# Attention heads on one core: V sums in two banks, later row maxima, a 128-row bias, and turned batch loops

## The chip, the cores and the metric

One core of a Trainium2 chip runs the whole program. The metric is the device time of one execution in microseconds, as the median over the runs that are shown. A shorter time is better. The core has five engines that run their own instruction streams and meet only at semaphores: TensorE (PE in the profile), VectorE (DVE), ScalarE (ACT), GpSimd (POOL) and SyncE (SP), which here only issues transfers.

## The reference, cut to what matters

The input is 8 sequences of 1024 rows of 256 numbers. A first layer (a selective scan, with its layer norm) is not touched by the change. The second layer is:

```
qkv = x @ W_qkv + b_qkv            # 16 heads of 16 columns
p = softmax(q @ k.T / sqrt(16))    # per head, 1024 x 1024
attn_out = p @ v
gate = softmax(x @ W_gate + b_gate); keep the two largest of 8
moe_out = sum_e gate_e * (x @ W_experts[e] + b_experts[e])
x = layernorm(x + attn_out + moe_out)
```

## The kernel before, in words

The kernel has two phases. The scan takes the first half of the time. The attention phase then goes through 8 batches (one sequence each), and each batch has an experts stage and a heads stage. Each engine has a Python-unrolled body for these stages inside a hardware loop over batches: `experts(0)` stands ahead of the loop, the loop body is `heads(b)` and then `experts(b + 1)`, and the last `heads` stands behind it. On VectorE the loop over heads 1 to 13 is a hardware loop as well.

**A step** is one head. It has eight rounds, `kt` 0 to 7. In a round TensorE makes the two halves of the transposed scores of key tile `kt` (`scores_t`, L1043) into two PSUM banks by turns, and ScalarE turns each half into probabilities (`exp_unit`, L1247). Beside them TensorE makes the untransposed scores of the head two steps ahead (`scores`, L1026), of which VectorE takes the row maxima (`take_max`, L1372). The sums of probabilities times V (`weigh_v`, L1056) accumulate over the eight key tiles in PSUM bank 6. Tiles 0 to 4 are summed in rounds 3 to 7 of the head's own step. Tiles 5 to 7 are late: tile 5 is summed in round 0 of the next step, tiles 6 and 7 both in round 1.

**The sums on their way out.** ScalarE copies the finished sums of the head before out of PSUM (`take_o`, L1254) after the first exponential of round 2. TensorE turns them in round 6 (`turn_o`, L1068) into bank 7, and VectorE divides by the row sums (`normalise`, L1379 and L1381). Since bank 6 is the only one for sums, `weigh_v` of tile 0 waits until `take_o` is done.

**The maxima on their way in.** The row maxima of the next head must be subtracted inside the score matmul, as two more rows of `q_st`. TensorE turns them (`turn_max`, L1035) at the end of round 3 into bank 7. ScalarE copies them (`take_max`, L1260) after the first exponential of round 4. SyncE then issues four small transfers of `m_rows` into `q_st` (L948). The first `scores_t` of the next step waits for all four (semaphore `s_md`, L1041).

**The experts stage.** TensorE makes 32 units of six 512-column matmuls each (L1163). ScalarE scales the odd units (L1305) and GpSimd adds them (L1006), VectorE adds the even ones (L1494 to L1504). Behind sixteen of the units 13 to 31 (the tuple `EARLY`) TensorE also makes one tile of scores of heads 0 and 1 (L1026), and VectorE takes its maxima. At the end ScalarE waits for the last GpSimd sum before its first exponential, since both use the same memory.

**The projections** of the next batch (`qk_proj`, L1088) run inside steps 14 and 15. Each half ends with a matmul of two rows (L1090) that adds the bias.

Of the kernel before, what the change touches and what calls it, by code (L numbers as in the profile page):

```python
# [24 lines left out]
P = 128  # L25
NB = 8
# [719 lines left out]
def attention_phase(nc, d):  # L746
    with ExitStack() as ctx:
# [50 lines left out]
        b_one = sb("b_one", [2, HALF], F16)  # L798
# [15 lines left out]
        r_sum = sb("r_sum", [P, 2, QUARTERS, 1])  # L814
# [79 lines left out]
        EARLY = tuple(u for u in range(13, EU) if u % 2 or u in (16, 20, 22, 24, 26, 28))  # L894
# [5 lines left out]
        block = ctx.enter_context(nc.Block())  # L900

# [76 lines left out]
        def _(pool):  # L978
# [4 lines left out]
            pool.memset(b_one[:, :], Q_UP)  # L983
            pool.memset(eps_col[:, :], EPS).then_inc(s_const, 1)
            pool.wait_ge(s_const, 1)
            pool.memset(k_st[QR - HD:RG, :, :], Q_UP).then_inc(s_const, 1)
# [28 lines left out]
        def _(pe):  # L1015
# [15 lines left out]
            def turn_max(b, h, normalised):  # L1031

                pe.wait_ge(s_nm, normalised + 1)
                pe.wait_ge(s_mp, b * HEADS + h + 1)
                pe.transpose(ps[0:2 * TT, 7, 0:P], m_parts[:, :, :].rearrange("p c t -> p (c t)"), ident[:, :]).then_inc(s_mt, 1)  # L1035
# [10 lines left out]
            def weigh_v(b, h, kt):  # L1046

                g = b * HEADS + h
                pe.wait_ge(s_p, g * (2 * TT) + (2 * kt + 4))
                if kt in (0, 5):  # L1050
                    pe.wait_ge(s_vh, g * 2 + (1 + kt // 5))
                if kt == 0:
                    pe.wait_ge(s_o, g + 1)
                n = T // QUARTERS
                for j in range(QUARTERS):
                    mm = pe.matmul(ps[VC * j:VC * (j + 1), 6, 0:n], v_h[:, kt, :], probs[:, kt, j * n:(j + 1) * n],  # L1056
                                   start=(kt == 0), stop=(kt == TT - 1), skip_group_check=True)
                mm.then_inc(s_pv, 1)

            def turn_o(b, h, turned=False):  # L1060

                g = b * HEADS + h
                if turned:
                    pe.wait_ge(s_mr, g + 4)
                pe.wait_ge(s_o, g + 2)
                pe.wait_ge(s_nm, g + 1)
                for i in range(2):
                    mm = pe.transpose(ps[:, 7, i * P:(i + 1) * P], o_sb[:, i * P:(i + 1) * P], ident[:, :])  # L1068
                mm.then_inc(s_ot, 1)
# [10 lines left out]
            def qk_proj(b, n, half):  # L1080

                mt = SEQ[n]
                if n == 0:
                    pe.wait_ge(s_xte, (b + 1) * KH)
                if n >= 2:
                    pe.wait_ge(s_parts, b * (2 * KH) + (n - 1))
                for i, (k, w, x) in enumerate(TERMS):
                    pe.matmul(ps[:, 2 * (n % 2) + half, :], w_qk[:, w, k, mt * P:(mt + 1) * P],  # L1088
                              x1T[:, x, k, half * HALF:(half + 1) * HALF], start=(i == 0), stop=False)
                mm = pe.matmul(ps[:, 2 * (n % 2) + half, :], b_st[0:2, mt * P:(mt + 1) * P], b_one[:, :], start=False, stop=True)  # L1090
                if half == 1:
                    mm.then_inc(s_qk, 1)
# [12 lines left out]
            def step(b, h, before, ahead, front):  # L1105
# [3 lines left out]
                for kt in range(TT):  # L1109
# [40 lines left out]
            def experts(b):  # L1150
                for t in range(4, TT):
                    v_proj(b, t)
                for t in range(TT):
                    for e2 in range(E // 2):
# [3 lines left out]
                        if u == 3:  # L1158
# [7 lines left out]
                        if u in EARLY:  # L1166
                            unit = EARLY.index(u)
# [3 lines left out]
                            for half in range(2):  # L1171
                                scores(b, unit // TT, unit % TT, 1 - half)
                            if unit == TT + 4:
                                turn_max(b, 0, b * HEADS)
# [44 lines left out]
        def _(act):  # L1219
# [30 lines left out]
            def take_o(b, h):  # L1250
# [3 lines left out]
                act.activation(o_sb[:, :], ps[:, 6, 0:T // QUARTERS], ACT.Copy).then_inc(s_o, 1)  # L1254

            def take_max(b, h):
# [3 lines left out]
                act.activation(m_rows[:, :], ps[0:2 * TT, 7, 0:P], ACT.Copy).then_inc(s_mr, 1)  # L1260
# [67 lines left out]
        def _(dve):  # L1328
# [45 lines left out]
            def normalise(b, h):  # L1374
                g = b * HEADS + h
                o = ps[:, 7, 0:2 * P].rearrange("p (i j c) -> p i j c", i=2, c=VC)
                to = att[:, :, ds(h * HD, HD)].rearrange("p (j i) c -> p i j c", i=2)
                dve.wait_ge(s_ot, g + 2)
                dve.reciprocal(r_sum[:, :, :, :], o[:, :, :, HD:HD + 1]).then_inc(s_rc, 1)  # L1379
                dve.wait_ge(s_rc, g + 1)  # L1380
                dve.tensor_tensor(to, o[:, :, :, 0:HD], r_sum[:, :, :, :].broadcast_to([P, 2, QUARTERS, HD]),  # L1381
# [53 lines left out]
            def experts(b, late):  # L1435
# [45 lines left out]
                for t in range(TT):  # L1481
                    if late is not None and t < 4:
                        add_experts(late, 2 * t, 2 * t + 2)
                    for e2 in range(E // 2):
# [14 lines left out]
                        if u in EARLY:  # L1499
                            unit = EARLY.index(u)  # L1500
                            take_max(b, unit // TT, unit % TT, unit >= TT)
# [92 lines left out]
            with dve.Fori(0, NB - 1) as b:  # L1594
                heads(b, True)
                experts(b + 1, b)
# [59 lines left out]
```

## Time and profile before

| | us |
|---|---|
| median of 3 runs | 4483.18 |
| lowest and highest | 4480.59, 4494.94 |
| the profiled execution | 4478.55 |
| its span | 4476.8 |
| PE, DVE, ACT busy | 3758.6, 3393.0, 2626.5 |
| chain of waits: PE | 33% |

The profile is of one execution. Busy times are unions over an engine's instructions. An engine's share of the whole span mixes the scan with the attention phase, so the rows below are of single stretches of the attention phase.

### The profile page before, as it was taken

What the parts mean: (1) busy time and instruction counts of PE and PEld (TensorE: products, weight loads), DVE (VectorE), ACT (ScalarE), POOL (GpSimd) and SP (SyncE); (2) the same over time, 40 slices, a digit from 0 to 9 for tenths busy, and PEclk for the clock granted to TensorE, in tenths of its full rate; (3) what the DMA queues carried; (4) which work ended last, traced back from release to release, by engine and by line L of the source; (5) the groups of instructions that cost most, each with busy time, mean ns of one, the idle gap of its engine ahead of it and who ended that gap; (6) DMA issues with size and microseconds to landing.
All of it is one profiled execution on the core that took longest, in us unless ns stands there. A gap on an engine that the chain in (4) does not pass through costs nothing.

```text
span 4476.8 us, 134619 instructions
## 1 busy us (share of the span) xinstructions
PE 3758.6 (84%) x52938; PEld 1752.8 (39%) x52938; DVE 3393.0 (76%) x3617; ACT 2626.5 (59%) x3840; POOL 1618.4 (36%) x1102
## 2 busy tenths in 40 slices
PE   6888878788877888888578988989889898898987
PEld 4445444454544445444332332323223232232322
DVE  6777767777677777777688788787887878788785
ACT  4545446454554545545228668485785857758587
POOL 4656746567465665756620020201102011020100
PEclk8899989999898998999889999999999999999998
DMA  3333334242342423434250230603205050050500
GB/s 104 106 88 97 101 82 115 78 115 73 97 115 73 115 74 99 121 77 108 79 76 11 44 53 2 95 2 59 39 3 94 2 73 25 18 79 2 83 5 11
DMA packets 143258, 301.00 MB, mean 67 GB/s; under 512 B 24344, under 2 KB 63904, under 8 KB 142432
## 3 DMA queue, kind: packets, MB, share of 16 engines
q1 hardware_dynamic: 142688, 292.60, 29.3%
q8 instruction: 455, 7.45, 0.7%
q14 instruction: 115, 0.94, 0.1%
HBM read 223.32 MB, written 35.13 MB: 58 GB/s over the span
## 4 chain that ended last, share of the span: by engine, by line
PE 33%; ACT 7%; issue 6%; DVE 3%; ACTq 1%; DMA 0%; SPq 0%; POOL 0%; DVEq 0%; POOLq 0%
PE ps L1056 10%; PE ps L1043 10%; PE ps L1163 6%; ACT probs L1247 6%; PE ps L1088 2%; PE ps L1026 1%; PE ps L1068 1%; PE ps L1101 1%; ACT o_sb L1254 1%; PE ps L1189 1%; PE ps L1035 1%; ACT m_rows L1260 1%; PE ps L1090 0%; DVE diag_b L1529 0%; ACTq L1246 0%
## 5 line engine op out<-in xcount | busy, mean ns | idle before, releaser
L335 POOL TENSOR_TENSOR z<-z,c_rep 128x1024 f32<-128x1024 f32 x512 | 1210.2, 2377 | 830.3 <-DVE z L720 829.8
L1247 ACT ACTIVATE probs<-ps,e_scale 128x512 f32<-128x512 f32 x2048 | 1295.5, 683 | 350.7 <-PE ps L1043 320.6
L720 DVE TENSOR_TENSOR_SCAN z<-dA,ps 128x1024 f32<-128x1024 f32 x512 | 1155.1, 2279 | 353.6 <-PE ps L386 333.2
L1372 DVE TENSOR_REDUCE neg_max<-ps 128x1 f32<-128x1024 f32 x1024 | 1236.8, 1222 | 173.5 <-PE ps L1026 145.7
L1043 PE MATMUL ps<-q_st,k_st 50*128 50x512 f16 x2048 | 717.5, 398 | 217.0 <-ACT probs L1247 182.2
L602 ACT ACTIVATE dA<-rep,a_rep 128x1024 f32<-128x1024 f32 x512 | 578.6, 1145 | 526.8 <-DVE z L720 519.4
L386 PE MATMUL ps<-diag,u_t 64*64 64x64 f32 x32768 | 635.5, 231 | 272.4 <-DVE z L720 197.6
L386 PEld LDWEIGHTS ps<-diag,u_t 64*64 64x64 f32 x32768 | 572.3, 144 | 516.0 <-issue 515.0
L1026 PE MATMUL ps<-k_st,q_st 48*128 48x512 f16 x2048 | 689.1, 395 | 0.1
L1056 PE MATMUL ps<-probs,v_h 128*32 128x256 f32 x8192 | 641.7, 399 | 0.0
L1012 POOL COPY v_h<-v_all 128x80 f32 (+1 forms) x256 | 62.2, 245 | 1502.5 <-PE ps L1056 1502.5
L405 PE MATMUL ps<-z,eye 128*64 128x512 f32 x2048 | 518.7, 629 | 3.4 <-POOL z L335 3.4
L1043 PEld LDWEIGHTS ps<-q_st,k_st 50*128 50x128 f16 x2048 | 179.0, 93 | 773.7 <-ACT probs L1247 657.9
L1163 PE MATMUL ps<-w_e,x1T 128*128 128x512 f16 x1536 | 360.4, 382 | 2.8 <-DVE acc L1504 2.8
L1006 POOL TENSOR_TENSOR x_in<-x_in,probs 128x256 f32<-128x256 f32 x256 | 192.5, 752 | 439.5 <-ACT probs L1305 427.6
L1056 PEld LDWEIGHTS ps<-probs,v_h 128*32 128x32 f32 x8192 | 177.2, 109 | 257.1 <-issue 230.0
L1305 ACT ACTIVATE probs<-ps,comb_s 128x256 f32<-128x256 f32 x256 | 106.5, 471 | 246.1 <-PE ps L1163 190.8
L405 PEld LDWEIGHTS ps<-z,eye 128*64 128x64 f32 x2048 | 130.2, 142 | 214.5 <-issue 183.7
L1163 PEld LDWEIGHTS ps<-w_e,x1T 128*128 128x128 f16 x1536 | 140.6, 98 | 183.0 <-issue 32.2
L1026 PEld LDWEIGHTS ps<-k_st,q_st 48*128 48x128 f16 x2048 | 173.9, 93 | 55.4 <-issue 40.8
L417 PE MATMUL ps<-w_io,s_res 128*128 128x256 f32 x576 | 141.7, 391 | 1.3 <-DVE s_res L688 1.3
L369 PE MATMUL ps<-ident,sp_w 128*64 128x128 f32 x1024 | 88.7, 346 | 61.7 <-DVE sp_w L667 61.7
(175 smaller groups left out, 3288.4 us busy)
## 6 DMA issues: line engine op xcount, KB each, us to landing
c_rep<-c_scratch SPq DMA_DIRECT2D x512, 256.0 KB, 4.0
rep<-delta SPq DMA_DIRECT2D x128, 256.0 KB, 5.9
q_st<-qk_halves SPq DMA_DIRECT2D x192, 128.0 KB, 10.2
k_st<-qk_halves SPq DMA_DIRECT2D x192, 128.0 KB, 11.0
qk_halves<-qk_parts SPq DMA_DIRECT2D x32, 512.0 KB, 10.4
x_nat<-in_x SPq DMA_DIRECT2D x9, 1024.0 KB, 7.6
x_rows<-x_nat SPq DMA_DIRECT2D x9, 1024.0 KB, 6.0
xT<-in_xT SPq DMA_DIRECT2D x8, 1024.0 KB, 5.2
```

Source lines behind the costliest of these rows:

```text
L335: pool.tensor_tensor(z[:, k % ZR, :], z[:, k % ZR, :], c_rep[:, slot, :], ALU.mult).then_inc(s_zc, 1)
L386: mm = pe.matmul(ps[q * QD:(q + 1) * QD, 2 + 2 * (k % 2) + r, i * TB:(i + 1) * TB], u_t[rows, i, m * P + j * QD:m * P + (j + 1) * QD], dia ...
L405: mm = pe.matmul(ps[j * QD:(j + 1) * QD, half, :], eye[:, :], z[:, (grp * QN + j) % ZR, half * HALF:(half + 1) * HALF], start=False, stop= ...
L602: act.activation(dA[:, k % AR, :], rep[:, slot, :], ACT.Exp, scale=a_rep[:, m, j, g:g + 1]).then_inc(s_da, 1)
L720: dve.tensor_tensor_scan(z[:, k % ZR, :], dA[:, k % AR, :], pair(1 + k % 2), 0.0, ALU.mult, ALU.add).then_inc(s_z, 1)
L1006: pool.tensor_tensor(to, to, scaled[:, i % 2, e, :], ALU.add).then_inc(s_pa, 1)
L1026: mm = pe.matmul(ps[:, 2 * (qt % 2) + half, :], head(q_st, half, QR, h, qt * P, P), head(k_st, half, QR, h, half * HALF, HALF), start=True ...
L1043: pe.matmul(ps[:, 4 + half, :], head(k_st, half, QM, h, kt * P, P), head(q_st, half, QM, h, half * HALF, HALF), start=True, stop=True).the ...
L1056: mm = pe.matmul(ps[VC * j:VC * (j + 1), 6, 0:n], v_h[:, kt, :], probs[:, kt, j * n:(j + 1) * n], start=(kt == 0), stop=(kt == TT - 1), sk ...
L1163: mm = pe.matmul(ps[:, EBANK[u], :], x1T[:, x, k, t * P:(t + 1) * P], w_e[:, w, k, e2 * 2 * H:(e2 + 1) * 2 * H], start=(i == 0), stop=(i = ...
L1247: act.activation(probs[:, kt, half * HALF:(half + 1) * HALF], ps[:, 4 + half, :], ACT.Exp, scale=e_scale[:, h:h + 1]).then_inc(s_p, 1)
L1372: dve.tensor_reduce(neg_max[:, qt:qt + 1], pair(qt % 2), AX.X, ALU.max, negate=True).then_inc(s_mx, 1)
```

## The change

The diff does six things. Sums of probabilities times V go to bank 6 for even heads and bank 7 for odd heads (`o_bank`), are turned within their own bank, and the turned maxima of head h go to the bank of head h's parity (`max_bank`; head 0 uses bank 7). `weigh_v` of tile 0 waits for `normalise` of the head two before instead of `take_o`. The three late tiles stand in rounds 0, 1 and 2. `take_o` moves behind the first exponential of round 4, `turn_max` to the end of round 4, and ScalarE's `take_max` behind the second exponential of round 5. The bias matmul has 128 rows (those behind the first two are zero in `b_one`). The early maxima come two tiles at a time behind eight units. ScalarE's and VectorE's batch loops begin with `experts` and end with `heads`; TensorE's, GpSimd's and SyncE's stay. VectorE's loop over heads is unrolled.

```diff
-        b_one = sb("b_one", [2, HALF], F16)
+        b_one = sb("b_one", [P, HALF], F16)
...
-        EARLY = tuple(u for u in range(13, EU) if u % 2 or u in (16, 20, 22, 24, 26, 28))
+        EARLY = (13, 15, 18, 20, 22, 24, 26, 28)
...
+        def o_bank(h):
+            return 6 + h % 2
+        def max_bank(h):
+            return 6 + h % 2 if h else 7
...
-            def turn_max(b, h, normalised):
-                pe.wait_ge(s_nm, normalised + 1)
+            def turn_max(b, h):
+                if h >= 2:
+                    pe.wait_ge(s_o, b * HEADS + h)
                 pe.wait_ge(s_mp, b * HEADS + h + 1)
...
-                if kt == 0:
-                    pe.wait_ge(s_o, g + 1)
+                if kt == 0 and h >= 2:
+                    pe.wait_ge(s_nm, g)
...
-                mm = pe.matmul(..., b_st[0:2, mt * P:(mt + 1) * P], b_one[:, :], ...)
+                mm = pe.matmul(..., b_st[:, mt * P:(mt + 1) * P], b_one[:, :], ...)
...
-                    if before and kt < 2:
+                    if before and kt < 3:
                         weigh_v(b, h - 1, 5 + kt)
-                    if before and kt == 1:
-                        weigh_v(b, h - 1, TT - 1)
                     if kt >= 3:
                         weigh_v(b, h, kt - 3)
-                    if turned and kt == 3:
-                        turn_max(b, h + 1, b * HEADS + h - 1 if before else b * HEADS)
+                    if turned and kt == 4:
+                        turn_max(b, h + 1)
...
-                            for half in range(2):
-                                scores(b, unit // TT, unit % TT, 1 - half)
+                            for half in range(4):
+                                scores(b, unit // TT, unit % TT + half // 2, 1 - half % 2)
...
-                        if before and kt == 2 and half == 0:
+                        if before and kt == 4 and half == 0:
                             take_o(b, h - 1)
-                        if turned and kt == 4 and half == 0:
+                        if turned and kt == 5 and half == 1:
                             take_max(b, h + 1)
...
-            with act.Fori(0, NB - 1) as b:
+            heads(0)
+            with act.Fori(1, NB) as b:
+                experts(b, b - 1)
                 heads(b)
-                experts(b + 1, b)
-            heads(NB - 1)
...
-                with dve.Fori(1, HEADS - PRE) as h:
+                for h in range(1, HEADS - PRE):
                     step(b, h, True)
...
-            with dve.Fori(0, NB - 1) as b:
+            heads(0, True)
+            with dve.Fori(1, NB - 1) as b:
+                experts(b, b - 1)
                 heads(b, True)
-                experts(b + 1, b)
+            experts(NB - 1, NB - 2)
             heads(NB - 1, False)
```

## Rows read from the trace of the kernel before

**Rows 1.** The page: engines' busy time, share of the span, and instructions.

```profile
PE 3758.6 (84%) x52938; PEld 1752.8 (39%) x52938; DVE 3393.0 (76%) x3617; ACT 2626.5 (59%) x3840; POOL 1618.4 (36%) x1102
```

**Rows 2.** Stretches: one step of batch 1; the start of its step 0.

```profile
core 0: us, PE busy (x) PEld busy (x) DVE busy (x) ACT busy (x) POOL busy (x), PEclk, DMA share, GB/s
...
2711.57:2723.55 11.98, 10.53 (x101) 3.39 (x99) 10.35 (x15) 10.32 (x18) 0.48 (x2) 1.00 0.01 2
...
2624.60:2634.80 10.20, 9.30 (x49) 2.08 (x49) 7.56 (x10) 7.35 (x13) 0.00 (x0) 0.50 0.22 78
```

**Rows 3.** Timeline of one step; start, length, engine, line, count [idle before].

```profile
2709.64 0.39 PE L1043 MATMUL ps<-q_st,k_st 50*128 50x512 f16 x1
...
2711.11 0.39 PE L1043 MATMUL ps<-q_st,k_st 50*128 50x512 f16 x1
...
2711.61 1.27 ACT L1247 ACTIVATE probs<-ps,e_scale 128x512 f32<-128x512 f32 x2 [0.20 <-PE ps L1043]
...
2712.79 0.39 PE L1043 MATMUL ps<-q_st,k_st 50*128 50x512 f16 x1
...
2713.88 0.38 ACT L1254 ACTIVATE o_sb<-ps 128x256 f32<-128x256 f32 x1
2714.03 0.39 PE L1043 MATMUL ps<-q_st,k_st 50*128 50x512 f16 x1 [0.64 <-ACT probs L1247]
...
2714.14 1.85 ACT L1247 ACTIVATE probs<-ps,e_scale 128x512 f32<-128x512 f32 x3
...
2715.98 0.39 PE L1043 MATMUL ps<-q_st,k_st 50*128 50x512 f16 x1
...
2717.07 0.25 ACT L1260 ACTIVATE m_rows<-ps 16x128 f16<-16x128 f32 x1
...
2717.23 0.39 PE L1043 MATMUL ps<-q_st,k_st 50*128 50x512 f16 x1
...
2721.62 0.39 PE L1043 MATMUL ps<-q_st,k_st 50*128 50x512 f16 x1
```

**Rows 4.** Chain of waits around the start of step 2, batch 1.

```profile
2644.66 0.26 ACT m_rows L1260
...
2647.24 2.10 DMA q_st<-m_rows
...
2649.46 0.40 PE ps L1043
```

**Rows 5.** Chain of waits, experts to heads: into the loop, then over its edge.

```profile
2350.30 0.80 POOL x_in L1006
2351.38 0.70 ACT probs L1247
...
2620.65 0.79 POOL x_in L1006
...
2624.22 0.70 ACT probs L1247
```

**Rows 6.** Timeline, VectorE and TensorE, at both ends of the loop body.

```profile
2565.71 0.26 ACT L1298 ACTIVATE gate<-gate 128x64 f32<-128x64 f32 x1 [6.48 <-DVE gate L1444]
...
2575.76 1.04 PE L1181 MATMUL ps<-ident,comb 128*8 128x128 f32 x8 [0.89 <-DVE acc L1504]
...
2624.91 0.17 DVE L1357 TENSOR_SCALAR m_rest<-neg_max 128x8 f32<-128x8 f32 x1 [3.01 <-issue]
```

**Rows 7.** Timeline, TensorE at the early maxima and at the bias matmul.

```profile
2614.32 1.47 PE L1163 MATMUL ps<-w_e,x1T 128*128 128x512 f16 x6
...
2615.72 0.39 PE L1026 MATMUL ps<-k_st,q_st 48*128 48x512 f16 x2
...
2616.05 2.76 PE L1163 MATMUL ps<-w_e,x1T 128*128 128x512 f16 x12
...
2550.28 1.47 PE L1088 MATMUL ps<-x1T,w_qk 128*128 128x512 f16 x6
...
2551.68 0.38 PE L1090 MATMUL ps<-b_one,b_st 2*128 2x512 f16 x1
```

More of the change, by code:

```diff
@@ L813, in attention_phase @@
         o_sb = sb("o_sb", [P, T // QUARTERS])
-        r_sum = sb("r_sum", [P, 2, QUARTERS, 1])
+        r_sum = sb("r_sum", [P, 2, 2, QUARTERS, 1])
         att = sb("att", [P, TT, H])
@@ L982, in _ @@
             pool.memset(tiny[:, :], 1e-30)
-            pool.memset(b_one[:, :], Q_UP)
-            pool.memset(eps_col[:, :], EPS).then_inc(s_const, 1)
+            pool.memset(eps_col[:, :], EPS)
+            pool.memset(b_one[:, :], 0.0).then_inc(s_const, 1)
             pool.wait_ge(s_const, 1)
+            pool.memset(b_one[0:2, :], Q_UP)
             pool.memset(k_st[QR - HD:RG, :, :], Q_UP).then_inc(s_const, 1)
@@ L1051, in weigh_v @@
                     pe.wait_ge(s_vh, g * 2 + (1 + kt // 5))
-                if kt == 0:
-                    pe.wait_ge(s_o, g + 1)
+                if kt == 0 and h >= 2:
+                    pe.wait_ge(s_nm, g)
                 n = T // QUARTERS
                 for j in range(QUARTERS):
-                    mm = pe.matmul(ps[VC * j:VC * (j + 1), 6, 0:n], v_h[:, kt, :], probs[:, kt, j * n:(j + 1) * n],
+                    mm = pe.matmul(ps[VC * j:VC * (j + 1), o_bank(h), 0:n], v_h[:, kt, :], probs[:, kt, j * n:(j + 1) * n],
                                    start=(kt == 0), stop=(kt == TT - 1), skip_group_check=True)
@@ L1065, in turn_o @@
                 pe.wait_ge(s_o, g + 2)
[L1066 removed]
                 for i in range(2):
[L1068 removed]
+                    mm = pe.transpose(ps[:, o_bank(h), i * P:(i + 1) * P], o_sb[:, i * P:(i + 1) * P], ident[:, :])
                 mm.then_inc(s_ot, 1)
@@ L1089, in qk_proj @@
                               x1T[:, x, k, half * HALF:(half + 1) * HALF], start=(i == 0), stop=False)
-                mm = pe.matmul(ps[:, 2 * (n % 2) + half, :], b_st[0:2, mt * P:(mt + 1) * P], b_one[:, :], start=False, stop=True)
+                mm = pe.matmul(ps[:, 2 * (n % 2) + half, :], b_st[:, mt * P:(mt + 1) * P], b_one[:, :], start=False, stop=True)
                 if half == 1:
@@ L1157, in experts @@
                             used(b, EPREV[u])
-                        if u == 3:
+                        if u == 2:
                             pe.wait_ge(s_nm, b * HEADS + 1)
@@ L1166, in experts @@
                         if u in EARLY:
-                            unit = EARLY.index(u)
+                            unit = 2 * EARLY.index(u)
                             if unit == 0:
@@ L1170, in experts @@
                                 pe.wait_ge(s_eba, (b + 1) * 5)
-                            for half in range(2):
-                                scores(b, unit // TT, unit % TT, 1 - half)
+                            for half in range(4):
+                                scores(b, unit // TT, unit % TT + half // 2, 1 - half % 2)
                             if unit == TT + 4:
-                                turn_max(b, 0, b * HEADS)
+                                turn_max(b, 0)
                     if t == 1:
@@ L1253, in take_o @@
                 act.wait_ge(s_ot, g + 1)
-                act.activation(o_sb[:, :], ps[:, 6, 0:T // QUARTERS], ACT.Copy).then_inc(s_o, 1)
+                act.activation(o_sb[:, :], ps[:, o_bank(h), 0:T // QUARTERS], ACT.Copy).then_inc(s_o, 1)
             def take_max(b, h):
@@ L1259, in take_max @@
                 act.wait_ge(s_md, g * 64 + 16)
-                act.activation(m_rows[:, :], ps[0:2 * TT, 7, 0:P], ACT.Copy).then_inc(s_mr, 1)
+                act.activation(m_rows[:, :], ps[0:2 * TT, max_bank(h), 0:P], ACT.Copy).then_inc(s_mr, 1)
             def step(b, h, before, turned):
@@ L1499, in experts @@
                         if u in EARLY:
-                            unit = EARLY.index(u)
-                            take_max(b, unit // TT, unit % TT, unit >= TT)
+                            unit = 2 * EARLY.index(u)
+                            for unit in (unit, unit + 1):
+                                take_max(b, unit // TT, unit % TT, unit >= TT)
                         if e2 % 2 == 0:
```

8 lines of the change are left out of this document (4 added, 4 removed).

## The prediction

> **What bounds the kernel now.** I read the page first. TensorE is busy 84% of the span and VectorE 76% [rows 1]. Those shares mix several stages, so I went to stretches. A middle step takes 11.98 us, in which TensorE, VectorE and ScalarE are busy 10.53, 10.35 and 10.32 us at full granted clock [rows 2]. None of the three is full: they hand work to each other. Steps 2 to 13 of the first seven batches repeat this length nearly to the hundredth. So I read one step as a timeline, start by start of the first L1043 of each round [rows 3]: 2709.64, 2711.11, 2712.79, 2714.03, then 2715.98, and 2721.62 begins the next step.
>
> Three kinds of round are to be seen. Round 2 has no late tile and takes 1.24 us (2712.79 to 2714.03): score, 0.50 us later its exponential (2711.11 to 2711.61), 0.69 us of that, and the bank is free. Round 0 has one tile of sums and takes 1.47 us, because TensorE reaches the next score late. After a long round the exponential comes late enough that the next one is short even with a tile in it: round 4 has one and takes 1.25 us (2715.98 to 2717.23). Round 1 has two tiles and takes 1.68 us. Round 3, which meets `take_o`, one tile and `turn_max`, takes 1.95 us [rows 3].
>
> Then I looked for what else ends at a step's start. `scores_t` of round 0 waits for four small transfers that begin with `take_max`. The chain of waits at the start of step 2 shows them whole: `take_max` ends at 2644.92, SyncE issues the fourth transfer at 2647.24, it lands 2.10 us later at 2649.34, and the score starts at 2649.46 [rows 4]. That is 4.54 us. In the step of rows 3, `take_max` ends at 2717.32 and the next step starts 4.30 us later at 2721.62. So the transfers take at most 4.30 us there, and they end hardly before the last exponential that the start also needs. The kernel stands close to the edge of this transfer already.
>
> **The steps.** I lay the new order out with the same round lengths. Spread tiles make rounds 0 to 3 alternate: 1.24 + 1.47 + 1.24 + 1.47 = 5.42 us, against 6.34 before (2709.64 to 2715.98); `take_o` and `turn_max` have left them. In round 4 the first exponential starts at 5.92. Exponentials follow each other every 0.58 us (1.27 for two, less 0.69) [rows 3]. So `take_o` starts at 6.51 and ends at 6.89. The second exponential starts 0.26 after its start, at 6.77 (2713.88 to 2714.14). `turn_max` now has a new wait, for `take_o`, since it writes that bank. Queued behind it on TensorE is the next score, and ScalarE waits for that. TensorE is past its tile at about 6.7, waits to 6.95, and starts round 5 at 7.16. The two exponentials start at 7.66 and 8.25, and `take_max` runs from 8.83 to 9.08. Before, its end stood at 7.68 (2717.32 less 2709.64). Rounds 5 to 7 end the work at 7.16 + 1.25 + 1.8 + 1.25 = 11.5 us, where 1.8 is a long round and about 0.35 for `turn_o`. By the engines alone a step would fall by 0.5 us.
>
> But the transfers start behind `take_max`, and SyncE's part is unchanged. Their length is bounded by 2.32 us (the fourth lands as it is issued) and 4.54 us (step 2) [rows 4]. I take 4.2, near the 4.30 that a usual step allows. The next step then starts at 9.08 + 4.2 = 13.28 us. TensorE stands idle for 1.8 us, since everything behind the waiting score is queued in order: the next scores, their maxima, the sums. The two banks buy nothing, as the wait that they remove was not the last.
>
> - 13 starts (steps 2 to 14) in 8 batches: 104 x 1.30 = **+135**. Between nothing (ends at 2.32) and 104 x 1.64 = 171.
> - Step 0 has no late tiles and a slower clock. Its `take_max` is three exponentials later (1.8 us), partly behind slack: 8 x 1.0 = **+8** (0 to 14). The transfers for step 15 land behind the projections of step 14: 0.
> - Granted clock. At the start of step 0, behind an idle stretch, it was 0.50, and a TensorE instruction took 9.30/49 = 0.19 us against 10.53/101 = 0.104 [rows 2]. No row shows a stop of 1.8 us in every step. If it halves the clock for the first two rounds of a step, their 1.8 us of scores and sums grow by 1.4, half behind ScalarE: 0.8 at most. I take one step in three: 104 x 0.25 = **+26** (0 to 83).
>
> **The batch loops.** Entering the loop, ScalarE's first exponential came 0.28 us after the last GpSimd sum (2351.10 to 2351.38). Over the loop's edge it came 2.78 us after it (2621.44 to 2624.22) [rows 5]; there are six such edges. Turning the loop gives 6 x 2.5 = **-15**. ScalarE's edge then falls into 6.48 us of idle time ahead of the gates [rows 6] and is free. VectorE stalled too, for 3.01 us [rows 6]. Its edge moves between the last `normalise` and `take_v` of tile 4, the head of the gate chain. At its end TensorE already waits 0.89 us for VectorE [rows 6], so nothing covers it: the gates, the combine weights and the expert sums are queued behind. Five edges x 2.8 = **+14**, and TensorE's longer stop may halve the clock: **+2** (0 to 8). If the stall were covered there, 14 would be saved.
>
> The stall is seen at one place only in this trace. The Trainium skill (Runtime: NRT & Kernel Launch, Instruction fetch mechanics) says that a taken branch to a target outside the small window of loaded instructions must fetch it first. By that rule the stall moves with the branch, and the sum keeps its 14; if it belonged to the place, the time would be 14 less.
>
> Unrolling VectorE's head loop drops a short branch in each step, beside a wait for TensorE: 0. Its longer code may stall once more per batch; I take 0 (0 to +8).
>
> **Experts.** A unit with an early tile takes 1.73 us (2614.32 to 2616.05). Twelve matmuls without one take 2.76 less the tail of the last, 1.30 per unit, so a tile costs 0.43. Two together cost 0.31 + 0.22 + 0.32 - 0.22 = 0.63 (2614.32 to 2615.72 less five pitches of 0.216, and 0.33 back) [rows 7]. That is 0.23 saved in 8 units of 8 batches, 15 us. VectorE must take two maxima in a row, and the unit three later waits for its sum, so I take **-10** (0 to -15).
>
> **Bias rows.** The two-row matmul starts 0.10 us late (1.40 from the first of six, six pitches being 1.30) [rows 7]. It may be lost after it too where another projection follows. 8 halves x 7 x 0.10, and 8 x 0.2 once, make 7; some lies beside ScalarE: **-5** (0 to -7). The other wait, of u = 2 for `normalise`, comes 1.3 us earlier in work that is done by then: 0.
>
> **Sum.** 135 + 8 + 26 - 15 + 14 + 2 - 10 - 5 = +155. The profiled execution took 4478.55 us (its span is 4476.8), 4.6 below the median, within the spread of the runs shown. So 4634.
>
> **Rivals.**
> - *The clock holds at full speed.* For it: TensorE works again at once. Against: nothing like this stop is in the trace at full clock. 4634 - 28 = 4606.
> - *The clock halves in nearly every step.* 4634 + 57 = 4691. For it: the 0.50 of step 0 came with little TensorE work, not only with none.
> - *The transfers are hidden, and the kernel is faster.* It decides at one point: if they are in place within 2.4 us of the end of `take_max` (11.5 less 9.08), steps fall to 11.5. 4478.6 - 52 - 15 + 14 - 10 - 5 = 4411. Against: the chain shows 2.10 us for the last transfer alone, and three are issued before it. For it: only one step shows them whole.
> - *Both sides cancel*: transfers of 2.9 us. 4470 to 4492.
>
> **How the numbers follow.** Forecast 0.42 (its own range 4605 to 4665), clock holds 0.27, clock halves mostly 0.20, hidden transfers 0.08, cancelled 0.03. The range of 8 in 10 goes from transfers of 4.1 us with no clock loss (about 4580) to the halved clock (4700). A change of less than 0.3%, 13 us, can't be told from none here. Faster 0.08, same 0.03, slower 0.89.
>
> **What would show it.** In the profile after: starts of steps 13.2 to 13.7 us apart; the waits of L1043 on the transfer of `m_rows` in about 100 places, 1.8 us each; `take_max` at 8.8 us in the step; ScalarE's first exponential of batches 1 to 6 within 0.4 us of GpSimd; VectorE idle 3 us ahead of L1430. Steps of 11.5 us would prove me wrong. So would a stall that is gone on VectorE.

## The result and the profile after

| | us |
|---|---|
| before, median of 4 runs | 4481.89 (4475.99 to 4494.94) |
| after, median of 4 runs | 4820.71 (4814.95 to 4829.84) |
| ratio after to before | 1.0751, interval 1.0728 to 1.0774 |
| the profiled execution after | 4821.76 (span 4819.9) |

The change makes the kernel 7.5% slower. The sign was forecast, the size was not: +155 us were forecast, and the profiled executions differ by 343.

The page of after answers [rows 1]: the engines' busy time hardly moved, except that TensorE took 198 us more for the same 52938 matmuls. Work that is the same and takes longer points at the clock.

```profile
span 4819.9 us, 133645 instructions
...
PE 3956.9 (82%) x52938; PEld 1747.2 (36%) x52938; DVE 3406.6 (71%) x3617; ACT 2636.9 (55%) x3840; POOL 1618.3 (34%) x1103
...
PEclk9989999898989989897889888898898897888888
```

The next view answers [rows 2]: two neighbouring steps of batch 1, the first at full granted clock, the second partly at half. The third line is a part of the second in which the clock is mostly low (it stood at 0.50 from 2703.18 to 2710.00); the columns are those of [rows 2].

```profile
core 0: us, PE busy (x) PEld busy (x) DVE busy (x) ACT busy (x) POOL busy (x), PEclk, DMA share, GB/s
2717.57:2730.70 13.13, 10.87 (x99) 3.30 (x100) 10.50 (x14) 10.37 (x18) 0.48 (x2) 1.00 0.01 2
2702.03:2717.57 15.54, 13.25 (x100) 3.30 (x100) 10.50 (x14) 10.41 (x18) 0.48 (x2) 0.78 0.01 2
...
2702.10:2709.90 7.80, 7.80 (x52) 1.72 (x52) 5.04 (x6) 5.06 (x8) 0.22 (x1) 0.57 0.00 0
```

Both steps have the same instructions. The one at full clock takes 13.13 us against 11.98 before. The other takes 15.54, and TensorE is busy 2.38 us longer in it. In the part with the low clock TensorE has no idle time at all (7.80 busy of 7.80): there it has become the bound.

The timeline answers [rows 3]: the first L1053 of a round, what ScalarE does for the change, and the first score of the next step.

```profile
2717.56 0.38 PE L1053 MATMUL ps<-q_st,k_st 50*128 50x512 f16 x1 [1.72 <-DMA q_st<-m_rows]
...
2718.81 0.39 PE L1053 MATMUL ps<-q_st,k_st 50*128 50x512 f16 x1
...
2720.28 0.39 PE L1053 MATMUL ps<-q_st,k_st 50*128 50x512 f16 x1
...
2721.52 0.39 PE L1053 MATMUL ps<-q_st,k_st 50*128 50x512 f16 x1
...
2722.99 0.39 PE L1053 MATMUL ps<-q_st,k_st 50*128 50x512 f16 x1
...
2724.08 0.38 ACT L1261 ACTIVATE o_sb<-ps 128x256 f32<-128x256 f32 x1
...
2726.38 0.25 ACT L1267 ACTIVATE m_rows<-ps 16x128 f16<-16x128 f32 x1
...
2730.70 0.38 PE L1053 MATMUL ps<-q_st,k_st 50*128 50x512 f16 x1 [1.72 <-DMA q_st<-m_rows]
```

The chain of waits over the end of that step answers [rows 4].

```profile
2726.49 0.15 ACT m_rows L1267
...
2726.76 0.61 SPq L956
...
2727.50 0.60 SPq L956
...
2728.23 0.59 SPq L956
...
2728.96 1.62 DMA q_st<-m_rows
...
2730.70 0.40 PE ps L1053
```

And one line of TensorE's waits over the whole run: us in total, times, longest.

```profile
PE ps L1053 <- DMA q_st<-m_rows: 195.9, 115, 2.3
```

The rounds are as laid out: 1.25, 1.47, 1.24 and 1.47 us. `take_max` starts 8.82 us into the step (forecast 8.83), SyncE issues a transfer every 0.73 us, the fourth needs 1.62, and the next step starts 4.07 us after the end of `take_max` (forecast 4.2). TensorE stands idle for 1.72 us (forecast 1.8). The starts of steps 2 to 14 all wait like this, 104 of the 115 places, 1.74 us on average.

The second place where time went is the edge of VectorE's loop, in the chain of waits from the heads of batch 1 into the experts of batch 2, and in the timeline there. An edge is the branch back to the start of a loop's body; its cost is counted here from the start of the branch to the next instruction of that engine's stream. Before, VectorE stood idle for 3.01 us at it [rows 6].

```profile
2901.46 0.06 DVEq L1603
2901.52 11.28 issue
...
2912.91 0.10 DVE v_all L1437
```

```profile
2912.91 0.48 DVE L1437 SCALAR_TENSOR_TENSOR v_all<-ps,r_w,b_vg 128x256 f32<-128x256 f32 x1 [11.25 <-issue]
...
2915.16 6.84 PE L1170 MATMUL ps<-w_e,x1T 128*128 128x512 f16 x24 [6.50 <-DVE gate L1439]
...
2915.65 0.26 ACT L1305 ACTIVATE gate<-gate 128x64 f32<-128x64 f32 x1 [17.44 <-DVE gate L1451]
```

VectorE does nothing for 11.25 us behind the branch at L1603, and waits for nothing that the profile shows. TensorE then waits 6.50 us and ScalarE 17.44. ScalarE's own edge lies under that wait.

**Where the time went.** Both profiled executions, cut at ScalarE's exponentials: a step runs from one head's first exponential to the next head's, a gap from the last exponential of a batch to the first of the next.

| part | before | after | difference |
|---|---|---|---|
| up to the first exponential | 2351.4 | 2357.0 | +5.7 |
| step 0, 8 batches | 107.1 | 118.3 | +11.2 |
| steps 1 to 13, 104 in all | 1247.0 | 1501.8 | +254.8 |
| steps 14 and 15 | 286.6 | 277.0 | -9.6 |
| 7 gaps (experts and edges) | 462.6 | 542.3 | +79.7 |
| behind the last exponential | 22.2 | 23.4 | +1.1 |

The first line is nearly all scan, which no kernel here changes, and it lies between 2337.7 and 2361.1 us in the profiled executions of all of them: its +5.7 is no effect of the change that could be told.

From the first exponential to the end TensorE's granted clock stood at 0.50 for 146 us before and for 659 us after. In steps 1 to 13 it never fell before. After, it was at 0.50 there for 435 us, in 95 of the 104 steps. In the gaps it was at 0.50 for 7 us before and 89 after.

### The profile page after: what moved, and what is told of

Its sections match the earlier page's. It is cut to its first block, busy times and chain, and to the rows that moved or that the text cites. A ratio compares the mean times of both kernels' runs of the same rounds, so it can differ in the third digit from the quotient of the medians.

```text
span 4819.9 us, 133645 instructions
## 1 busy us (share of the span) xinstructions
PE 3956.9 (82%) x52938; PEld 1747.2 (36%) x52938; DVE 3406.6 (71%) x3617; ACT 2636.9 (55%) x3840; POOL 1618.3 (34%) x1103
## 4 chain that ended last, share of the span: by engine, by line
PE 25%; issue 8%; ACT 6%; DVE 5%; SPq 5%; DMA 4%; ACTq 1%; DVEq 0%; POOL 0%; POOLq 0%
PE ps L1066 8%; PE ps L1053 8%; SPq L956 5%; ACT probs L1254 4%; DMA q_st<-m_rows 4%; PE ps L1170 3%; PE ps L1097 2%; PE ps L1035 2%; DVE neg_max L1379 1%; PE ps L1045 1%; PE ps L1196 1%; ACT o_sb L1261 1%; PE ps L1110 0%; DVE acc L1512 0%; DVE diag_b L1537 0%
## 5 line engine op out<-in xcount | busy, mean ns | idle before, releaser
L1053 PE MATMUL ps<-q_st,k_st 50*128 50x512 f16 x2048 | 810.5, 449 | 265.9 <-DMA q_st<-m_rows 195.9
L1035 PE MATMUL ps<-k_st,q_st 48*128 48x512 f16 x2048 | 757.5, 447 | 3.9 <-DVE neg_max L1379 3.1
L1066 PE MATMUL ps<-probs,v_h 128*32 128x256 f32 x8192 | 759.5, 450 | 0.0
L1053 PEld LDWEIGHTS ps<-q_st,k_st 50*128 50x128 f16 x2048 | 167.3, 95 | 880.8 <-ACT probs L1254 574.9
L1170 PE MATMUL ps<-w_e,x1T 128*128 128x512 f16 x1536 | 375.1, 400 | 46.9 <-DVE gate L1439 35.3
L1035 PEld LDWEIGHTS ps<-k_st,q_st 48*128 48x128 f16 x2048 | 160.6, 96 | 42.4 <-issue 25.4
L352 PE MATMUL ps<-xT,w_io 128*128 128x512 f32 x256 | 121.3, 615 | 22.4 <-DMA w_dt<-in_b_dt 13.2
```

The lines of the kernel that those rows point to most:

```text
L1035: mm = pe.matmul(ps[:, 2 * (qt % 2) + half, :], head(q_st, half, QR, h, qt * P, P), head(k_st, half, QR, h, half * HALF, HALF), start=True ...
L1053: pe.matmul(ps[:, 4 + half, :], head(k_st, half, QM, h, kt * P, P), head(q_st, half, QM, h, half * HALF, HALF), start=True, stop=True).the ...
L1066: mm = pe.matmul(ps[VC * j:VC * (j + 1), o_bank(h), 0:n], v_h[:, kt, :], probs[:, kt, j * n:(j + 1) * n], start=(kt == 0), stop=(kt == TT ...
L1170: mm = pe.matmul(ps[:, EBANK[u], :], x1T[:, x, k, t * P:(t + 1) * P], w_e[:, w, k, e2 * 2 * H:(e2 + 1) * 2 * H], start=(i == 0), stop=(i = ...
```

## The experiments

Three questions were open: whether the late `take_max` alone makes the stop and what part the clock has in it; why an edge costs 11 us and not 3; and which of the small edits helps. A ratio is always to the kernel before, run on the same chip beside it; "half clock" is the time at 0.50 from the first exponential to the end of the profiled execution (146 before, 659 after).

### Where take_max stands

**e1_early_max**: the changed kernel with the sums and maxima taken early again.

```diff
-                    if turned and kt == 4:
+                    if turned and kt == 3:
                         turn_max(b, h + 1)
...
-                        if before and kt == 4 and half == 0:
+                        if before and kt == 3 and half == 0:
                             take_o(b, h - 1)
-                        if turned and kt == 5 and half == 1:
+                        if turned and kt == 4 and half == 0:
                             take_max(b, h + 1)
```

> The changed kernel, with turn_max back at the end of round 3, take_max behind the first exponential of round 4, and take_o behind the first exponential of round 3 (where the bank that turn_max needs is free in time). Two banks, spread tiles, turned loops stay. If the late take_max and its four transfers set the step (my theory), steps fall to 11.5 to 11.8 us at full granted clock, and the time falls by 270 to 320 us from the changed kernel's 4821, to about 4520. If the longer steps come from something else in the new order (bank use, the spread tiles, the wait of tile 0 for normalise), the time stays above 4700.

Measured: 4486.13 us (10 runs), ratio 1.0009 (0.9994 to 1.0023). Steps 1 to 13 take 11.50 us on average, none of them at half clock (213 us in all), and the gaps are still 548.0. TensorE waits for the transfers 3 times in the attention phase, 3.8 us in all. One step of batch 1:

```profile
2707.72:2719.27 11.55, 10.88 (x101) 3.34 (x100) 10.18 (x15) 10.41 (x19) 0.48 (x2) 1.00 0.01 2
```

The three moves take back 335 us, somewhat more than the 270 to 320 expected. Since almost nothing waits for the transfers here, the 11.55 us are what the engines need in this order; two banks, spread tiles and the later `take_o` are together worth 0.43 us a step once the transfers do not end last. That the time equals the one before is a sum of opposite parts: in the profiled executions the steps 1 to 13 gain 51 us and steps 14 and 15 gain 23, and the gaps lose 85.

**e3_only_late_max**: the kernel before, with nothing changed but the place of `take_max`.

```diff
-                        if turned and kt == 4 and half == 0:
+                        if turned and kt == 5 and half == 1:
                             take_max(b, h + 1)
```

> The kernel before, with only ScalarE's take_max moved from behind the first exponential of round 4 to behind the second of round 5. Theory: the transfers alone set the step, 13.3 us at least, and each stop of TensorE lowers the granted clock as in the changed kernel: steps of 13.5 to 14.5 us, 4482 + 200 to 260 us, about 4710. Rival (the clock falls for another reason than the stop): steps of 13.3 us at full clock, about 4620. Rival (the late take_max is not the cause): below 4500.

Measured: 4713.89 us (5 runs), ratio 1.0517 (1.0499 to 1.0534). Steps 1 to 13 take 13.89 us on average, most of them 13.57; TensorE waits for the transfers 121 times, 195.3 us in all. This one line brings over two thirds of the loss. The transfers did what was expected, the clock did so only in part. Half clock is 268 us, 137 of them in steps 1 to 13, and there it touches 23 steps. The 78 steps with none of it take 13.58 us on average, though nearly every one begins with such a stop. The stops are about as many and as long as after's (195.3 / 121 = 1.61 us against 195.9 / 115 = 1.70), and after had 435 us of half clock in 95 steps. So a stop of this length does not lower the clock by itself every time. The profiled execution was also the fastest of the five (4679.77). Why the clock falls less here is open.

**e11_two_transfers**: the changed kernel with only the high halves of the maxima sent, two transfers a step. The score matmul has 49 rows instead of 50, and the shift inside the softmax is less exact.

```diff
-                for part in range(2):
+                for part in range(1):
...
...
-pe.wait_ge(s_md, g * 64 + 80)
+pe.wait_ge(s_md, g * 32 + 48)
```

> The changed kernel, with two of the four transfers of the maxima: the low half of each maximum is left out of q_st (49 rows in the score matmul, not 50), so the softmax shift is less exact. take_max stays late. Theory (the step waits for the chain of four transfers): with two fewer issues of 0.73 us the chain lasts 2.6 us, steps fall to 11.6 to 11.9 us at full clock, about 4560. Rival (take_max's place hurts in another way): steps stay over 13 us, above 4750.

Measured: 4509.18 us (4 runs), ratio 1.0059 (1.0036 to 1.0081). Steps take 11.65 us, none of them at half clock (189 us in all). The chain of waits for one step, and the timeline of the score behind the transfers of the step before:

```profile
2703.91 0.15 ACT m_rows L1267
...
2704.93 1.64 DMA q_st<-m_rows
```

```profile
2694.99 0.38 PE L1053 MATMUL ps<-q_st,k_st 49*128 49x512 f16 x1 [0.29 <-DMA q_st<-m_rows]
```

The time is 51 us under the 4560 expected. The late `take_max` is still there (8.81 us into the step), but two transfers land 2.52 us after its end (2704.05 to 2706.57) instead of the 3.95 of four (2726.63 to 2730.58). With that the stop shrinks from 1.72 us to 0.29 and the clock holds. So the place of `take_max` costs only through the four transfers behind it, but for the 0.15 us a step by which this kernel lies over e1. This is close to the point of 2.4 us that the prediction had named for its rival.

### The clock

**e4_filler**: the changed kernel with 14 more matmuls a step, behind the last sums of the step, where TensorE would stand idle. They write into the unused half of the sums' bank and disturb the sums that are open in it, so the numbers that this kernel computes are not right. The other engines work as before: VectorE and ScalarE are busy 10.49 and 10.36 us of a step, against 10.50 and 10.37 in after.

```diff
+                    if ahead and kt == TT - 1:
+                        for _ in range(14):
+                            pe.matmul(ps[:, o_bank(h), 2 * P:4 * P], x1T[:, 0, 0, 0:P], x1T[:, 0, 0, 0:2 * P], ...)
```

> The changed kernel, with 14 matmuls of 128 x 128 by 256 f16 columns more at the end of round 7 of steps 0 to 13, into the unused half of the bank of sums; nothing reads them. They fill 1.5 us of the 1.8 us stop. If the stop lowers the clock (theory), the half-clock stretches in the steps vanish, steps go to 13.1 to 13.4 us, and the time falls by 80 to 110 us to about 4725, though work is added. If the clock falls for another reason, or the fillers stand in the way of the score, the time is 4821 or more.

Measured: 4681.69 us (4 runs), ratio 1.0439 (1.0422 to 1.0457), so 139 us less than after, with more work, and more than the 80 to 110 that were expected. Half clock is 219 us, none of it in steps 1 to 13. A step:

```profile
2689.42:2702.55 13.13, 12.51 (x116) 4.61 (x114) 10.49 (x15) 10.36 (x19) 0.48 (x2) 1.00 0.01 2
```

All 104 steps now take 12.8 to 13.6 us, 13.13 on average, the length that the transfers set. TensorE is busy 12.51 us of it instead of 10.87. The transfers cost 13.13 - 11.99 = 1.14 us a step, 119 us; the rest, 14.44 - 13.13 = 1.31 us a step, 136 us, is the clock. After itself says the same: the four of its steps that have no half clock take 13.15 us. The gaps of e4 are 10 us longer than after's and its other parts 10 us shorter, so the whole saving is about that of the steps.

### The loop edges

**e2_loops_unturned**: the changed kernel with ScalarE's and VectorE's batch loops as they were; VectorE's head loop stays unrolled.

```diff
-            heads(0)
-            with act.Fori(1, NB) as b:
-                experts(b, b - 1)
-                heads(b)
+            with act.Fori(0, NB - 1) as b:
+                heads(b)
+                experts(b + 1, b)
+            heads(NB - 1)
```

(and the same for VectorE)

> The changed kernel, with ScalarE's and VectorE's batch loops as before (heads first, then experts); all else as changed. If the turned loop's edge costs the 14 us per batch that stand between heads and experts (my theory), that stretch falls from 80 to 66 us in five or six batches, at a price of 2.5 us at each edge on the other side: 55 to 70 us less, about 4760. If the stretch is longer for another reason (late normalise, clock), the time stays within 15 us of 4821.

Measured: 4747.27 us (4 runs), ratio 1.0581 (1.0561 to 1.06), 73 us less than after. The gaps fall from 542.3 to 481.3 us, and the edges cost 2.8 to 3.7 us again. The other 12 us lie in the steps (14.31 us on average against 14.44). They need not be the loops' doing: the steps 1 to 13 take 1485 to 1511 us in after, e2, e6, e9 and e13, which all have the same steps.

**e5_only_turned_loops**: the kernel before with both loops turned, VectorE's head loop still a loop.

```diff
-            with dve.Fori(0, NB - 1) as b:
+            heads(0, True)
+            with dve.Fori(1, NB - 1) as b:
+                experts(b, b - 1)
                 heads(b, True)
-                experts(b + 1, b)
+            experts(NB - 1, NB - 2)
             heads(NB - 1, False)
```

(and ScalarE's as in the change)

> The kernel before, with only ScalarE's and VectorE's batch loops turned to begin with the experts (VectorE's inner loop over heads stays a loop). Theory: the edge is cheap between experts and heads and costs 12 us between heads and experts, whatever the rest of the kernel does: the stretch between heads and experts grows by 10 to 14 us in six batches, 60 to 80 us in all, about 4555. My prediction's step (2.8 us at the new edge, 2.5 us saved at the old) would give 4484.

Measured: 4514.9 us (4 runs), ratio 1.0063 (1.004 to 1.0087), and so 40 us less than expected, and 31 more than the prediction's own prices would give. ScalarE's edge cost 12.75 to 13.19 us at all six places; VectorE's cost 0.33 us. The timeline at one edge, ScalarE's first instruction behind it:

```profile
2843.65 0.26 ACT L1298 ACTIVATE gate<-gate 128x64 f32<-128x64 f32 x1 [12.52 <-issue]
```

The six gaps with an edge are 74.9 to 75.2 us; before, they were 66.1 to 67.9 and the last 63.6. So ScalarE's edge alone costs some 9 us. The 6.48 us of idle time that were to hide it [rows 6] do not hold 12.52: VectorE, which had its part of the gates ready, waits 6.36 us for ScalarE's. TensorE's idle time grows by it too, from under 6 us in each gap to over 9, and its clock stands at 0.50 for 13.7 us in each of the six, where before five of them had under 1. At VectorE's edge the trace has no packet of an instruction queue between the branch and the next instruction, at any of the five places: there nothing was fetched. Why its code did not have to be fetched here, with the heads in a loop, is not shown.

**e13_act_unturned**: the changed kernel with ScalarE's loop alone as it was.

```diff
-            with act.Fori(1, NB) as b:
+            with act.Fori(0, NB - 1) as b:
...
```

> The changed kernel, with only ScalarE's batch loop as before; VectorE's stays turned. Theory (VectorE's long edge sets the stretch between heads and experts, and ScalarE's runs beside it): nothing is won there, ScalarE's edge of 2.6 us is paid again between experts and heads: 4821 + 10 to 20, about 4835. Rival (ScalarE's edge of 12 us is the one that binds): 4760 to 4790.

Measured: 4802.76 us (4 runs), ratio 1.0714 (1.069 to 1.0739), 18 us less than after, where 10 to 20 more were expected. The intervals of the two touch, and the profiled executions differ by 17 us in steps 1 to 13, which the edit does not change, so nothing is to be read from the size. The gaps tell more. At the five edges that VectorE has, they are 80.6 to 82.7 us, against 79.3 to 81.3 in after: nothing is won, and ScalarE's old edge of some 2.6 us is paid again. At the sixth, which only ScalarE had, the gap falls from 75.0 to 65.8. So VectorE's edge binds where both are, and ScalarE's binds where it is alone.

**e6_loads_held**: two theories stood for the 11 us. The one: instructions are fetched by DMA, and the fetch stands behind the data that the loads bring. The other: the longer code of the turned loops needs more fetches. In this kernel SyncE loads the stacks of the next batch and stores results just when heads end. Here half of those loads wait until VectorE has passed its edge (`s_gl` counts the gates).

```diff
+                        if c >= 2:
+                            sp.wait_ge(s_gl, b + 2)
```

> The changed kernel, with SyncE's loads of the last two quarters of the stacks (24 transfers of 128 KB for the next batch) held back until VectorE has shifted the gate logits of that batch, so that they do not run when the two engines branch back. Theory (fetching the code behind the branch waits for these loads): both edges fall from 12 us to about 3 us, and the time falls by 45 to 65 us from 4821, to about 4765. Rival (the edge is long because the loop body is long, or for its place): edges stay at 11 to 13 us and the time stays at 4821 or more.

Measured: 4810.48 us (4 runs), ratio 1.0733 (1.07 to 1.0766), no different from after. VectorE's edges stayed at 10.98 to 12.30 us. Inconclusive: other transfers on the same queue still filled the DMA engines at the edge (102% of their time in a stretch of 12 us around one edge).

**e9_all_loads_held**: the same wait for all of these loads.

```diff
+                        sp.wait_ge(s_gl, b + 2)
```

> The changed kernel, with SyncE's loads of all four quarters of the stacks held back until VectorE has shifted the next batch's gate logits, so that at the edge between heads and experts no large transfer runs. Theory (the code behind the branch waits for these transfers): the edges of VectorE and ScalarE fall from 12 us to 3 or 4 us. Rival (they are long for the place or length of the loop body): they stay at 11 to 13 us. The whole time says less, since the loads may then be late for the next heads: 4740 to 4850.

Measured: 4792.15 us (4 runs), ratio 1.0676 (1.065 to 1.0703), 29 us less than after. VectorE's edges cost 2.76 to 2.99 us, ScalarE's 2.40 to 2.68, in the same code. The DMA queues during the edge, first of after (2901.5 to 2913), then of this kernel (2910 to 2915); the columns are packets, MB and the share of the DMA engines' time:

```profile
q1 hardware_dynamic: 1144, 2.01, 101.3%
q14 instruction: 2, 0.02, 0.8%
q8 instruction: 1, 0.02, 0.5%
```

```profile
q8 instruction: 1, 0.02, 1.5%
q14 instruction: 3, 0.02, 1.5%
```

And VectorE's first instruction behind this kernel's edge, which now waits for TensorE:

```profile
2914.20 0.48 DVE L1438 SCALAR_TENSOR_TENSOR v_all<-ps,r_w,b_vg 128x256 f32<-128x256 f32 x1 [2.70 <-PE ps L1111]
```

The instruction queues move three and four packets. With 2 MB of data on the DMA engines the edge takes 11.3 us, with nothing beside it 2.8. The packets' times in the traces show where it goes. At VectorE's and ScalarE's edges with full DMA engines (after and e5), the last packet of queue 14 ahead of the engine's restart begins 8.9 to 10.9 us after the branch and takes 0.3 to 1.2 us. At all of e9's edges it begins 0.9 to 1.2 us after the branch. So what grows is the time ahead of the packet, and not the packet's own. (The record does not name the engine that a packet is for; the one meant here is the last ahead of each restart.) The first theory holds.

The gaps fall only to 73.7 to 75.4 us between batches 1 and 6, and not to e2's 69. The chain of waits from the experts into batch 3 shows one reason, first in after and then here:

```profile
2973.79 1.62 DMA q_st<-m_rows
```

```profile
2973.84 5.60 DMA q_st<-m_rows
```

The held loads now run where the four small transfers of head 0 do, and the first score waits for these. From the end of the copy to that score it takes 6.1 to 8.9 us in these five gaps, 7.9 on average, against 5.2 in after. That is some 3 of the 5 us; the rest is not located.

The Trainium skill (Runtime: NRT & Kernel Launch, Instruction fetch mechanics) says that a taken branch out of the loaded window waits for a DMA fetch before it goes on. The runs agree, but for VectorE's branch in e5, which fetched nothing, and add the price: 2.4 to 3.0 us with idle DMA engines (e9), 10.8 to 13.2 with full ones (after and e5).

### The small edits

**e7_only_bias_rows**: the kernel before with the bias matmul over 128 rows.

```diff
-        b_one = sb("b_one", [2, HALF], F16)
+        b_one = sb("b_one", [P, HALF], F16)
...
-b_st[0:2, mt * P:(mt + 1) * P], b_one
+b_st[:, mt * P:(mt + 1) * P], b_one
```

> The kernel before, with only the bias matmul over 128 rows. Theory: 0.10 us less ahead of each of 56 such matmuls inside the steps and 0.2 us at 8 in the first projection: 5 to 7 us less, partly hidden, 4484 to 4478. Rival: hidden behind ScalarE, no change that can be told.

Measured: 4472.89 us (12 runs), ratio 0.9978 (0.9966 to 0.999): -9 us, between -4 and -15. Forecast -5. The larger matmul starts 1.08 us after the first of five (2544.81 to 2545.89), which is five pitches of 0.216: the 0.10 us of delay is gone. In the profiled executions step 14 falls from 20.51 to 20.15 us where the clock does the same in both, and step 15 from 16.51 to 16.21, so some 5 us in the seven batches with projections, as forecast. The other parts move both ways with the granted clock (half clock falls from 41 to 10 us in steps 14 and 15 and grows from 7 to 47 in the gaps), and are not traced to the bias.

**e8_only_early_twos**: the kernel before with the early maxima in twos behind eight units.

```diff
-        EARLY = tuple(u for u in range(13, EU) if u % 2 or u in (16, 20, 22, 24, 26, 28))
+        EARLY = (13, 15, 18, 20, 22, 24, 26, 28)
```

> The kernel before, with only the early maxima in twos. My prediction: 10 us less (up to 15). Rival, from the stretch between heads and next heads, which is 69 us instead of 66 in the changed kernel with unturned loops: VectorE's two maxima in a row make the unit three later wait, and the experts stage gets longer by 1 to 3 us a batch, 8 to 20 us more.

Measured: 4496.99 us (12 runs), ratio 1.003 (1.0017 to 1.0042): +15 us (8 to 19), where -10 was forecast. VectorE and TensorE around one pair, in their timelines:

```profile
2596.96 2.34 DVE L1372 TENSOR_REDUCE neg_max<-ps 128x1 f32<-128x1024 f32 x2
```

```profile
2603.10 2.76 PE L1163 MATMUL ps<-w_e,x1T 128*128 128x512 f16 x12 [1.99 <-DVE acc L1505]
```

The pair of maxima holds VectorE for 2.34 us; with the layer norm behind it, the sums of the experts are taken late, and TensorE waits 1.99 us for a free bank. The saving of 0.23 us a pair had been worked out from TensorE's rows alone.

### The best of both

**e12_best**: two banks, spread tiles and bias rows, the order of e1, the loops of e2, and the early maxima one at a time. Beside the diffs of e1 and e2:

```diff
-        EARLY = (13, 15, 18, 20, 22, 24, 26, 28)
+        EARLY = tuple(u for u in range(13, EU) if u % 2 or u in (16, 20, 22, 24, 26, 28))
```

> Two banks, spread tiles and the bias over 128 rows, with turn_max at the end of round 3, take_o behind the first exponential of round 3, take_max behind the first of round 4; early maxima one by one and ScalarE's and VectorE's batch loops as before. Theory: steps of 11.55 us, heads 197 us instead of 207, the stretch between heads at 66 us: 4482 - 75 = about 4405. Rival (e1 gained its 11.55 us from the turned loops' other constants): 4440 or more.

Measured: 4416.1 us (5 runs), ratio 0.9843 (0.9824 to 0.9862), 62 to 79 us less than before, and 11 above the 4405 expected. Steps 1 to 13 take 11.52 us as expected. The gaps are 470.6, 8 us more than before, with 35 us of half clock in them against 7. Half clock is 135 us in all. A step:

```profile
2702.79:2714.34 11.55, 10.88 (x101) 3.30 (x99) 10.16 (x14) 10.40 (x19) 0.48 (x2) 1.00 0.01 2
```

## Why the prediction was right in sign and wrong in size

- **The steps, mechanism and length.** Right. (One step in each of the first seven batches took 12.26 us before and not 11.98, which the prediction passed over; it moves nothing.) The transfers end last, where the prediction put them: `take_max` at 8.82 (8.83), 4.07 us to the next start (4.2), a stop of 1.72 (1.8). Round 5 starts 7.16 us into the step, to the hundredth as laid out. At full clock that is 119 us for 104 steps, forecast 135. e3 shows that this one move is enough, e1 and e11 that without it or with half the transfers it is gone.
- **Granted clock: the term that was mis-sized.** The prediction took one step in three and 0.25 us a step, 26 us in all. It measured 1.31 us a step, 136 us (e4), and 95 of the 104 steps had half clock in them. Only about a dozen stayed near 13.1 us. The low clock does not end after two rounds: in the view of 2702.10 to 2709.90 it stays for almost half a step, and TensorE, busy for all of these 7.80 us, takes 7.80 / 52 = 0.15 us for an instruction against 10.87 / 99 = 0.11. The top of the term's range, 83 us, came from the same assumption. Step 0 of before had shown the half clock over 10 us with TensorE busy 91% of it [rows 2]; the length of that stretch was not used, and the rival's words that it "came with little TensorE work" do not fit these 91%. How many steps would be hit no row could say, and e3, with the same stops and 137 us of half clock in its steps, shows that it could not be had from the stops alone.
- **VectorE's edge: the other one.** Forecast 2.8 us, measured 10.8 to 13.1. That the stall moves with the branch was right here (it did not in e5); its price was read at a place [rows 6] where the DMA engines were idle as the edge began, and carried to one where they are full. Before's trace shows it: their busy share in tenths from 2620 to 2626 us, in 40 slices, with the edge from 2621.55 to 2624.67.

```profile
DMA  0000400000000000101008137989956899999999
```

Against e2, the gaps with turned loops are 61 us longer; the prediction had -15 + 14 + 2 for the loops. These 61 hold the clock's part too: half clock in the gaps is 89 us in after and 40 in e2, where the prediction had 2 us for it.
- **ScalarE's edge.** Forecast as free in 6.48 us of idle time. It is under VectorE's where both are, and binds at the sixth (75.0 us against 65.8 in e13).
- **ScalarE's entry into the heads.** Right in place. In after, its first exponential of batch 1 comes 0.58 us after the last GpSimd sum (2658.66 to 2659.24), where it was 2.78 [rows 5]; forecast 0.4. That gap, which has no turned edge, is 66.40 us against 68.74 in e2: -2.3, forecast -2.5.
- **Early twos.** Wrong in sign. +15 us alone (e8) against -10. The unit was priced by TensorE's matmuls [rows 7]; VectorE's two maxima in a row were named, and taken for half of the saving only.
- **Bias rows.** -9 against -5, of which some 5 are seen where they were forecast (e7).
- **Step 0.** +11 against +8.

By these, the profiled executions' difference is 119 + 136 + 11 + 61 + 18 (the twos by the gaps of e2 less those of before, 481.3 - 462.6) - 10 (steps 14 and 15) + 7 (start and end) = 342, of 343. Of the 188 us by which the forecast fell short, 110 are the clock in the steps, 60 the edges and 28 the twos; the steps at full clock, put 16 too high, stand against them. Of the rivals, "the clock halves in nearly every step" described best what happened in the steps, but its price, 26 + 57 = 83 us, was too low for the same reason. Hidden transfers (11.5 us a step) did not come, though e1 and e11 show that steps of 11.5 to 11.7 are what comes when the transfers are in time.

## What to carry to other kernels

Before an operation moves later, count what hangs behind it up to the wait that it feeds, here four issues and a landing of 4.1 us: the move is free only while that chain ends before the engines do. A stop of TensorE can cost more than its length: price it once for the stop and once for the stretch at half clock behind it, with a stretch as long as those that the trace shows, and give every step being hit a real chance (95 of 104 here, 23 in e3). Put the back edge of a loop where the DMA queues are empty, for an edge is a transfer too; and look at what the loads that are moved away from it then meet, as in e9.

## What was not expected of the hardware

- With stops of 1.7 us once in 13 us TensorE's granted clock stood at 0.50 for 435 us of steps 1 to 13. With 14 matmuls in each of the same stops it did not fall there at all (e4), nor with stops of 0.29 us (e11).
- The fetch behind a far branch shares the DMA engines with data: 2.8 us without other traffic, 11.3 with it (e9 and after), nearly all of the difference ahead of the packet and not in it. Six such edges cost ScalarE 12.75 to 13.19 us each in e5, and the branch of VectorE in the same kernel 0.33.
- Four small transfers from one engine's queue land 3.95 us after the end of the copy, two after 2.52: the second pair costs 1.4 us, the two issues of 0.73 each. With large loads beside them the last of the four took 5.60 us instead of 1.62 (e9).
- Open: why the clock fell for only 137 us in the steps of e3, with stops about as long as those of after, and why VectorE's branch in e5 had nothing to fetch.
